# Reordering the first microseconds of a four-layer transformer kernel: layer-norm statistics and x chunks moved into the attention loop

## The chip, the cores and the metric

The kernel runs on one core of a Trainium2 chip. The metric is the device time of one execution in microseconds; less is better. A core has five engines that each work through their own instruction list in order and meet at semaphores: TensorE (PE), VectorE (DVE), ScalarE (ACT), GpSimd (POOL) and SyncE (SP), which here sends nearly all DMAs.

## What is computed

The input x has 32 batches of 128 tokens with 128 features; ctx has the same shape. Four layers follow one another:

```python
x = x + L0_xattn(layernorm(x), ctx, ctx)            # 16 heads of 8, rotary embedding on Q and K
x = x + L0_ffn(layernorm(x))                        # ternary weights, 128 -> 512 -> 128
x = x + L1_xattn(layernorm(x), ctx, ctx, mask)      # 16 query heads, 4 key heads, masks, norm of the output
x = x + L1_ffn(layernorm(x))                        # 8 experts, one chosen for each token
```

Of this only the start of the first attention layer is touched:

```python
def _layernorm(x, axis=-1, eps=1e-05):
    m = jnp.mean(x, axis=axis, keepdims=True)
    v = jnp.var(x, axis=axis, keepdims=True)
    return (x - m) / jnp.sqrt(v + eps)
Q = apply_rope(Q, cos_q, sin_q)
K = apply_rope(K, cos_k, sin_k)
scores = jnp.einsum('bhqd,bhkd->bhqk', Q, K) / math.sqrt(D_K)
attn = jax.nn.softmax(scores, axis=-1)
out = jnp.einsum('bhqk,bhkd->bhqd', attn, V)
```

## The kernel before

One batch (128 tokens) is one tile of x, and x stays in on-chip memory in the tensor XR. Two batches make a pair, and projections are made by pairs; scores, softmax and the product with V are made by batches. Pair 0 is batches 0 and 1, and so on.

**The loop.** All engines run the same software pipeline, `body_loop` (L253 and after), over a step number t. Each engine has a function `step(t, j)` with j = t % 6; steps -4 to 5 are written out, steps 6 to 23 are a hardware loop, and the last ones are written out again. Steps -8 to -5 stand ahead of `body_loop` on each engine (`for t in range(-AHEAD, START)`), and with other instructions between them they are the prologue. An engine's step t does work for different batches. On a pair p, ScalarE normalises (`normalise`, L931) at step 2p-8, TensorE transposes and projects Q at step 2p-6 and K at step 2p-5 (L499, L514), VectorE multiplies the projections by the cosine and sine tables right after (`rotate`, L1281), GpSimd adds the two products in the same step (`whole`, L1090), ScalarE casts the sum to bf16 one step later (`high`, L874), and GpSimd makes the two lower pieces (`cut`, L1101 to L1104, at steps 2p-5 for Q and 2p-4 for K). SyncE then sends the "stack" of the pair: DMAs from on-chip memory to on-chip memory that copy the pieces into the tensor Qs (six DMAs, L365, and one that clears a row, L367) at step 2p-4, and into Ks (six DMAs, L376) at step 2p-3.

On a batch b, TensorE makes the scores in two halves at step b-2 (`scores`, L558) and VectorE takes the negated row maxima of each half (`maxima`, L1316). GpSimd splits the maxima into bf16 pieces at step b-1 (`split_max`, L1112 to L1117), TensorE transposes them (`max_transpose`, L634), ScalarE copies them out (`evac_max`, L909), and SyncE sends them into a row of the stack (`max_rows`, L382), the last thing of its step b-1. At step b TensorE makes the transposed scores (`scoresT`), ScalarE the exponentials, TensorE the product with V.

Within TensorE's step the order is: scores half 0, product with V of the batch before, scoresT half 0, `max_transpose(t+1)`, `out_transpose`, `regroup`, the projection of Q (even t) or K (odd t), scoresT half 1, scores half 1 of batch t+2, product with V. Within VectorE's step: `add_out`, maxima half 0 of batch t+2, `denominators`, `norm_out`, `rotate`, maxima half 1 of batch t+2. Within GpSimd's step: `split_max(t+1)`, `cut`, `whole`. Within SyncE's step: the stack of Q (even t) or of K and the next chunk of ctx (odd t), then `max_rows(t+1)`.

**The statistics.** The norm of the first layer needs mean and variance of each tile. They are made in five groups of tiles, `GROUPS = ((0, 2), (2, 8), (8, 16), (16, 24), (24, 32))`. VectorE's `x_group(g)` waits for the chunk of x (four chunks of eight tiles, 512 KB each), then makes `bn_stats` (L1577) and `bn_aggr` (L1580) for each tile; GpSimd's `x_group(g)` waits for VectorE's and makes the reciprocal root and the shift in four instructions (L1065 to L1073). `normalise` of pair p waits for the group that holds the pair.

**The prologue before.** VectorE: group 0, then the stacks Ks[0], Ks[1], Ks[2] are filled with ones (L1585), group 1 ahead of step -7, group 2 ahead of step -6, group 3 ahead of step -5, group 4 after it. GpSimd: group 0, Qs[0], Qs[1], Qs[2] are cleared (L1156), then groups 1 to 4 in the same places. SyncE: chunk 0 of x, the first weights, the first chunk of ctx, and after step -7 nineteen loads of other weights and the x chunks 1, 2 and 3 (L327). At step -4 it waits until all six stacks are filled (`stacks_cleared`, 6) and sends the first stack.

Of the kernel before, what the change touches and what calls it, by code (L numbers as in the profile page):

```python
# [1 line left out]

# [1 line left out]

# [7 lines left out]
BF16 = mybir.dt.bfloat16  # L12
# [3 lines left out]
B, S, D = 32, 128, 128  # L16
HEADS, DK = 16, 8
# [9 lines left out]
AHEAD = 8  # L27
START = -4
# [14 lines left out]
GROUPS = ((0, 2), (2, 8), (8, 16), (16, 24), (24, 32))  # L43
# [13 lines left out]
def build(nc, a, out):  # L57
    ctx = ExitStack()
    with ctx:
        def sb(name, shape, dt=F32):  # L60
            return ctx.enter_context(nc.sbuf_tensor(name, shape, dt))
# [3 lines left out]
        def sem(name):  # L65
            if name not in sems:
                sems[name] = ctx.enter_context(nc.semaphore(name))
            return sems[name]
# [64 lines left out]
        Qs = [sb(f"Qs{i}", [128, HEADS // 2, PAIR], BF16) for i in range(3)]  # L133
        Ks = [sb(f"Ks{i}", [128, HEADS // 2, PAIR], BF16) for i in range(3)]
# [66 lines left out]
        blank = sb("blank", [128, EXPERTS, RW])  # L201
# [8 lines left out]
        before = sb("before", [128, 128], BF16)  # L210
# [30 lines left out]
        X_CHUNKS = 4  # L241
# [5 lines left out]

        body = {}

        def run(step, t):  # L250
            body["i"] = t // BODY
            step(t, t % BODY)

        def run_early(step, p):

            if isinstance(p, int) and p >= PAIRS - EARLY:
                run(step, p - (PAIRS - EARLY) - AHEAD)

        def body_loop(eng, step, first=-AHEAD, before=None):


            for t in range(first, BODY):
                run(step, t)
            with eng.Fori(1, NB) as i:
                body["i"] = i
                for j in range(BODY):
                    step(i * BODY + j, j)
            for t in range(NB * BODY, B + 3):
                if before and t in before:
                    before[t]()  # L270
                run(step, t)
# [52 lines left out]
        def _(sp):  # L324
            def load_x_chunk(c):
                w = B // X_CHUNKS
                sp.dma_start(X[:, c * w:(c + 1) * w, :], xd[:, c * w:(c + 1) * w, :]).then_inc(sem(f"x_loaded{c}"), 16)  # L327
# [69 lines left out]
            step = attention(0)  # L397
            for t in range(-AHEAD, START):
                run(step, t)
                if t == -AHEAD + 1:  # L400
                    for dst, src in other_loads:
                        sp.dma_start(dst, src).then_inc(sem("weights_loaded"), 16)
                    for c in range(1, X_CHUNKS):
                        load_x_chunk(c)
            sp.wait_ge(sem("stacks_cleared"), 6)
            sp.wait_ge(sem("zeros_set"), 1)
            body_loop(sp, step, START)
            for dst, src in expert_loads:
                sp.dma_start(dst, src).then_inc(sem("experts_loaded"), 16)

# [4 lines left out]
            sp.dma_start(blank[:, :, 2 * D:RW], a["tails"][DUMMIES * 128:].rearrange("(e p) w -> p e w", p=128)  # L415
                         ).then_inc(sem("tails_loaded"), 16)
            body_loop(sp, attention(1))

            sp.wait_ge(sem("tails_loaded"), 16)
# [419 lines left out]
        def _(act):  # L839
# [189 lines left out]
            step = attention(0)  # L1029
            for t in range(-AHEAD, START):  # L1030
                run(step, t)
            act.wait_ge(sem("weights_loaded"), LOADED)
            body_loop(act, step, START)
            early = attention(1)
# [7 lines left out]
        def _(pool):  # L1042
# [20 lines left out]
            def x_shift(name, tiles, n, index):  # L1063

                nc.gpsimd.tensor_tensor(xrs[:, tiles], xmv[:, tiles, 1], powers[:, 5:6].broadcast_to([128, n]), ALU.add  # L1065
                                        ).then_inc(sem(name + "_rstd"), 1)
                pool.wait_ge(sem(name + "_rstd"), 3 * index + 1)
                nc.gpsimd.tensor_tensor(xrs[:, tiles], xrs[:, tiles], powers[:, 0:1].broadcast_to([128, n]), ALU.pow
                                        ).then_inc(sem(name + "_rstd"), 1)
                pool.wait_ge(sem(name + "_rstd"), 3 * index + 2)  # L1070
                nc.gpsimd.tensor_tensor(xsh[:, tiles], xmv[:, tiles, 0], xrs[:, tiles], ALU.mult).then_inc(sem(name + "_rstd"), 1)
                pool.wait_ge(sem(name + "_rstd"), 3 * index + 3)
                nc.gpsimd.tensor_tensor(xsh[:, tiles], zero[:, 0:n], xsh[:, tiles], ALU.subtract).then_inc(sem(name), 2)  # L1073

            def x_group(g):

                lo, end = GROUPS[g]
                pool.wait_ge(sem("x0_stats"), 2 * end)
                x_shift("shifted0", slice(lo, end), end - lo, g)
# [72 lines left out]

            step = attention(0)
            x_group(0)
            for i in range(3):
                nc.gpsimd.memset(Qs[i][:], 0.0).then_inc(sem("stacks_cleared"), 1)  # L1156
            for t in range(-AHEAD, START):
                if t > -AHEAD:
                    x_group(t + AHEAD)
                run(step, t)  # L1160
            for g in range(START + AHEAD, len(GROUPS)):
                x_group(g)
            body_loop(pool, step, START)
            pool.wait_ge(sem("gate_unit"), 2)
            nc.gpsimd.tensor_tensor(wgn[:, 1:2], wgn[:, 0:1], powers[0:EXPERTS, 4:5], ALU.pow).then_inc(sem("gate_norm"), 1)
            early = attention(1)
# [62 lines left out]
        def _(dve):  # L1229
# [342 lines left out]
            def x_group(g):  # L1572

                lo, end = GROUPS[g]
                dve.wait_ge(sem(f"x_loaded{lo // (B // X_CHUNKS)}"), 16)
                for t in range(lo, end):
                    nc.vector.bn_stats(xst[:, t, :], X[:, t, :]).then_inc(sem("x0_stats"), 1)  # L1577
                dve.wait_ge(sem("x0_stats"), lo + end)
                for t in range(lo, end):
                    nc.vector.bn_aggr(xmv[:, t, :], xst[:, t, :]).then_inc(sem("x0_stats"), 1)  # L1580

            step = attention(0)
            x_group(0)
            for i in range(3):
                nc.vector.memset(Ks[i][:], 1.0).then_inc(sem("stacks_cleared"), 1)  # L1585
            dve.wait_ge(sem("first_loaded"), FIRST_LOADED)
            for t in range(-AHEAD, START):
                if t > -AHEAD:
                    x_group(t + AHEAD)
                run(step, t)  # L1590
            for g in range(START + AHEAD, len(GROUPS)):
                x_group(g)
            dve.wait_ge(sem("zeros_set"), 1)

            FW = (F1[:], F2[:].rearrange("p c n -> p (c n)"))
# [34 lines left out]
                sum_weights()  # L1630
                scale_norm()

            body_loop(dve, step, START, {B - 1: weights_ready, B: quantize, B + 2: fold_norm})
            nc.vector.tensor_tensor(wgs[:, 0, :], wgr[:], wgr[:], ALU.mult).then_inc(sem("gate_unit"), 1)
            dve.wait_ge(sem("gate_unit"), 1)
            nc.vector.tensor_reduce(wgn[:, 0:1], wgs[:, 0, :], AX.X, ALU.add).then_inc(sem("gate_unit"), 1)
# [95 lines left out]
```

## Time and profile before

| | |
|---|---|
| median of 3 runs | 695.83 us (694.47 to 696.17) |
| the profiled execution's own time | 697.29 us |
| its span in the profile | 695.5 us |
| PE busy | 561.4 us, 81% |
| DVE busy | 395.1 us, 57% |
| ACT busy | 353.4 us, 51% |
| POOL busy | 377.9 us, 54% |

The span runs from the first to the last instruction; what lies around it is 1.8 us. Times in the rows of the trace are microseconds from the start of the span. "Busy" counts the engine's own work, not waits or the issuing of DMAs, which is why SyncE ("SPq" in the trace, the queue from which it issues) has no share above. PE is TensorE's matmul row; two levels of its clock appear, and the share granted is shown in the views by stretch. Layer 0's attention fills the span from its start to about 223 us.

### The profile page before, as it was taken

What the parts mean: (1) busy time and instruction counts of PE and PEld (TensorE: products, weight loads), DVE (VectorE), ACT (ScalarE), POOL (GpSimd) and SP (SyncE); (2) the same over time, 40 slices, a digit from 0 to 9 for tenths busy, and PEclk for the clock granted to TensorE, in tenths of its full rate; (3) what the DMA queues carried; (4) which work ended last, traced back from release to release, by engine and by line L of the source; (5) the groups of instructions that cost most, each with busy time, mean ns of one, the idle gap of its engine ahead of it and who ended that gap; (6) DMA issues with size and microseconds to landing.
All of it is one profiled execution on the core that took longest, in us unless ns stands there. A gap on an engine that the chain in (4) does not pass through costs nothing.

```text
span 695.5 us, 19876 instructions
## 1 busy us (share of the span) xinstructions
PE 561.4 (81%) x6015; PEld 371.0 (53%) x6016; DVE 395.1 (57%) x1105; ACT 353.4 (51%) x839; POOL 377.9 (54%) x785
## 2 busy tenths in 40 slices
PE   1477989899875899959999999999882880499993
PEld 0345656666543799823444444444431450499993
DVE  6556667777765566434666666666643548044441
ACT  2136666776663456524655566565441520266662
POOL 6766556766710566645565655655324177255653
PEclk9999999999998799968999999999996855599997
DMA  6243333334327400022223222222100024233331
GB/s 185 77 108 87 98 95 90 101 97 104 96 51 233 113 2 0 17 80 73 64 59 80 70 58 69 77 56 62 39 7 2 9 104 158 75 93 94 98 99 31
DMA packets 97518, 54.02 MB, mean 78 GB/s; under 512 B 23138, under 2 KB 93538, under 8 KB 97458
## 3 DMA queue, kind: packets, MB, share of 16 engines
q1 hardware_dynamic: 94674, 46.45, 25.7%
q0 software_dynamic: 2784, 6.82, 2.7%
q8 instruction: 31, 0.51, 0.3%
q14 instruction: 29, 0.24, 0.1%
HBM read 19.79 MB, written 8.81 MB: 41 GB/s over the span
## 4 chain that ended last, share of the span: by engine, by line
PE 49%; SPq 24%; DVE 7%; POOL 6%; issue 6%; ACT 4%; DMA 2%; POOLq 0%; ACTq 0%; DVEq 0%
SPq L376 9%; SPq L365 9%; PE score L535 6%; PE scoreT L535 5%; PE bank L808 5%; PE bank L610 4%; ACT P L893 4%; PE scoreT L693 4%; DVE negmax L1316 4%; PE bank L703 4%; PE score L558 3%; PE scoreT L576 3%; PE scoreT L796 3%; SPq L382 2%; POOL expert_rows L1205 2%
## 5 line engine op out<-in xcount | busy, mean ns | idle before, releaser
L1316 DVE TENSOR_REDUCE negmax<-score 128x8 f32<-128x1024 f32 x128 | 156.5, 1223 | 96.9 <-PE score L558 76.6
L893 ACT ACTIVATE P<-scoreT 128x1024 f32<-128x1024 f32 x128 | 131.1, 1024 | 62.7 <-PE scoreT L576 42.6
L610 PE MATMUL bank<-P,Vc 128*32 128x128 f32 x2048 | 83.2, 281 | 0.4
L558 PE MATMUL score<-Ks,Qs 64*128 64x128 bf16 x1024 | 52.7, 224 | 18.9 <-DMA Ks<-piece 8.6
L558 PEld LDWEIGHTS score<-Ks,Qs 64*128 64x128 bf16 x1024 | 31.7, 97 | 56.1 <-issue 47.9
L1220 POOL DMA_INDIRECT out<-by x39 | 39.6, 1017 | 37.5 <-POOL by L1214 22.6
L610 PEld LDWEIGHTS bank<-P,Vc 128*32 128x32 f32 x2048 | 48.5, 110 | 14.3 <-ACT P L893 1.0
L1112 POOL TENSOR_TENSOR negp<-negmax,blank 128x16 bf16<-128x16 f32 x64 | 14.0, 219 | 74.8 <-DVE negmax L1316 74.8
L899 ACT COPY outs<-bank 128x256 f32<-128x256 f32 x64 | 23.7, 371 | 58.5 <-PE bank L610 58.5
L1101 POOL TENSOR_TENSOR piece<-full,piece 128x256 bf16<-128x256 f32 x64 | 42.8, 668 | 16.6 <-ACT piece L874 16.5
L535 PE MATMUL score<-mask,negI 128*128 128x512 bf16 x128 | 40.9, 403 | 11.0 <-issue 5.9
L1104 POOL TENSOR_TENSOR piece<-rest,piece 128x256 bf16<-128x256 f32 x64 | 44.5, 695 | 5.0
L1205 POOL DMA_INDIRECT expert_rows<-XR,sloti x32 | 32.4, 1013 | 25.0 <-DVE sloti L1489 15.9
L535 PE MATMUL scoreT<-negI,mask 128*128 128x512 bf16 x128 | 39.6, 392 | 7.2 <-ACT P L893 6.6
L808 PE MATMUL bank<-M,bhT 128*128 x312 | 44.2, 285 | 0.3 <-ACT bhT L1021 0.3
L1102 POOL TENSOR_TENSOR rest<-full,piece 128x256 f32<-128x256 f32 x64 | 42.7, 667 | 0.0
L874 ACT CAST piece<-full 128x256 bf16<-128x256 f32 x64 | 25.6, 400 | 32.6 <-DMA Qs<-blank 12.0
L808 PEld LDWEIGHTS bank<-M,bhT 128*128 128x128 f32 x312 | 38.6, 195 | 1.5 <-issue 0.4
L1021 ACT ACTIVATE bhT<-scoreT,Qs 128x128 f32<-128x128 f32 x104 | 29.7, 369 | 16.4 <-PE scoreT L796 16.4
L1551 DVE SCALAR_TENSOR_TENSOR by<-bank,XB 128x128 f32<-128x128 f32 x39 | 13.7, 351 | 42.1 <-PE bank L808 40.7
L1325 DVE RECIPROCAL rden<-bank 128x16 f32<-128x16 f32 x64 | 16.3, 255 | 36.5 <-PE bank L625 36.5
L1090 POOL TENSOR_TENSOR full<-rotA,rotB 128x256 f32<-128x256 f32 x32 | 23.2, 727 | 25.1 <-DVE rotB L1281 25.1
(195 smaller groups left out, 1236.0 us busy)
## 6 DMA issues: line engine op xcount, KB each, us to landing
Qs<-piece SPq DMA_DIRECT2D x192, 64.0 KB, 2.0
Ks<-piece SPq DMA_DIRECT2D x96, 64.0 KB, 2.0
ctxT<-in_ctxT SPq DMA_DIRECT2D x32, 128.0 KB, 2.3
XB<-expert_rows SPq DMA_DIRECT2D x39, 66.0 KB
XA<-expert_rows SPq DMA_DIRECT2D x39, 64.0 KB, 1.9
XR<-in_x SPq DMA_DIRECT2D x4, 512.0 KB, 4.8
Qs<-blank SPq DMA_DIRECT2D x32, 64.0 KB, 2.1
Qs<-negpT SPq DMA_DIRECT2D x64, 32.0 KB, 1.9
```

Source lines behind the costliest of these rows:

```text
L365: sp.dma_start(rows_of(Qs[b], s), piece[0][:, QSLOT[s], :]).then_inc(sem(f"q_stacked{L}{b}"), 16)
L376: sp.dma_start(rows_of(Ks[b], s)[:, 0:n_kv // 2, :], piece[1][0:n_kv * DK, KSLOT[s], :]).then_inc(sem(f"k_stacked{L}{b}"), 16)
L535: nc.tensor.matmul(out[:, r, :].rearrange("p (h n) -> p h n", h=HQ), of_stationary, of_moving.unsqueeze(1).broadcast_to([128, HQ, 128]), s ...
L558: mm = nc.tensor.matmul(SCORE[:, r, i * 128:(i + 1) * 128], Qs[pb][rows, h, tb * S:(tb + 1) * S], Ks[pb][rows, kv, tb * S:(tb + 1) * S], s ...
L610: mm = nc.tensor.matmul(PVOUT[VCOL * i:VCOL * (i + 1), half * 128:(half + 1) * 128], Vc[:, k % BODY, at:at + VCOL], P32[:, c, i * 128:(i + ...
L808: mm = nc.tensor.matmul(bank[4 + r][:, 0:D], bhT[r][:, c * 128:(c + 1) * 128], M2[:, bass.ds(e, 1), c:c + 1, :].rearrange("p o c n -> p (o ...
L893: nc.scalar.activation(P32[:, half * 2:half * 2 + 2, :], SCORET[:], ACT.Exp, scale=SCALE).then_inc(sem("exp_done"), 1)
L1101: nc.gpsimd.tensor_tensor(pc[0:m, 1, :], f, h, ALU.subtract).then_inc(sem(f"{nm}_pieces"), 1)
L1102: nc.gpsimd.tensor_tensor(r, f, h, ALU.subtract).then_inc(sem(f"{nm}_pieces"), 1)
L1104: nc.gpsimd.tensor_tensor(pc[0:m, 2, :], r, pc[0:m, 1, :], ALU.subtract).then_inc(sem(f"{nm}_pieces"), 1)
L1205: nc.gpsimd.indirect_dma_start(out=rows_d, out_offset=bass.IndirectOffsetOnAxis(ap=sloti[:, t:t + 1], axis=0), in_=XR[:, t, :], in_offset= ...
L1316: nc.vector.tensor_reduce(negmax[:, k % 2, :, half * HQ:(half + 1) * HQ], SCORE[:].rearrange("p r (h k) -> p r h k", h=HQ), AX.X, ALU.max, ...
```

## The change

- `body_loop` now also looks into its table `before` in the steps -4 to 5 (it did so only in the last ones).
- The statistics: group 1 is made right after group 0 on VectorE and GpSimd. The groups 2, 3 and 4 are made ahead of the steps 0, 2 and 4 on both engines (`later_groups`).
- SyncE sends the x chunks 1, 2 and 3 ahead of its steps -2, 0 and 2.
- VectorE fills Ks[0] and Ks[1] ahead of its steps and Ks[2] after step -6. GpSimd clears Qs[0] and Qs[1]; ScalarE clears Qs[2] after its step -6 with a copy of 2048 bf16 zeros.

The same instructions are executed as before, except that one GpSimd memset has become a ScalarE copy with a wait for the zeros.

```diff
+        def later_groups(x_group):
+
+            return {2 * g - 4: partial(x_group, g) for g in range(2, len(GROUPS))}
...
             for t in range(first, BODY):
+                if before and t in before:
+                    before[t]()
                 run(step, t)
...
                     for dst, src in other_loads:
                         sp.dma_start(dst, src).then_inc(sem("weights_loaded"), 16)
-                    for c in range(1, X_CHUNKS):
-                        load_x_chunk(c)
             sp.wait_ge(sem("stacks_cleared"), 6)
             sp.wait_ge(sem("zeros_set"), 1)
-            body_loop(sp, step, START)
+            body_loop(sp, step, START, {2 * c - 4: partial(load_x_chunk, c) for c in range(1, X_CHUNKS)})
...
             for t in range(-AHEAD, START):
                 run(step, t)
+                if t == -AHEAD + 2:
+                    act.wait_ge(sem("zeros_set"), 1)
+                    nc.scalar.copy(Qs[2][:].rearrange("p h s -> p (h s)"),
+                                   blank[:].rearrange("p e w -> p (e w)")[:, 0:HEADS * S // 2].bitcast(BF16)).then_inc(sem("stacks_cleared"), 1)
...
             x_group(0)
-            for i in range(3):
+            x_group(1)
+            for i in range(2):
                 nc.gpsimd.memset(Qs[i][:], 0.0).then_inc(sem("stacks_cleared"), 1)
             for t in range(-AHEAD, START):
-                if t > -AHEAD:
-                    x_group(t + AHEAD)
                 run(step, t)
-            for g in range(START + AHEAD, len(GROUPS)):
-                x_group(g)
-            body_loop(pool, step, START)
+            body_loop(pool, step, START, later_groups(x_group))
...
+            def clear(i):
+                nc.vector.memset(Ks[i][:], 1.0).then_inc(sem("stacks_cleared"), 1)
+
             x_group(0)
-            for i in range(3):
-                nc.vector.memset(Ks[i][:], 1.0).then_inc(sem("stacks_cleared"), 1)
+            x_group(1)
+            clear(0)
+            clear(1)
             dve.wait_ge(sem("first_loaded"), FIRST_LOADED)
             for t in range(-AHEAD, START):
-                if t > -AHEAD:
-                    x_group(t + AHEAD)
                 run(step, t)
-            for g in range(START + AHEAD, len(GROUPS)):
-                x_group(g)
+                if t == -AHEAD + 2:
+                    clear(2)
...
-            body_loop(dve, step, START, {B - 1: weights_ready, B: quantize, B + 2: fold_norm})
+            body_loop(dve, step, START, {**later_groups(x_group), B - 1: weights_ready, B: quantize, B + 2: fold_norm})
```

## Rows read from the trace of the kernel before

**Rows 1.** The page, part 4: the chain that ended last, by engine and line.
```profile
PE 49%; SPq 24%; DVE 7%; POOL 6%; issue 6%; ACT 4%; DMA 2%; POOLq 0%; ACTq 0%; DVEq 0%
SPq L376 9%; SPq L365 9%; PE score L535 6%; PE scoreT L535 5%; PE bank L808 5%; PE bank L610 4%; ACT P L893 4%; PE scoreT L693 4%; DVE negmax L1316 4%; PE bank L703 4%; PE score L558 3%; PE scoreT L576 3%; PE scoreT L796 3%; SPq L382 2%; POOL expert_rows L1205 2%
```

**Rows 2.** The chain of waits, 0 to 110 us: start, duration, what.
```profile
12.66 4.12 DMA XR<-in_x
16.80 1.65 DVE xst L1577 x8
...
27.86 1.65 POOL xrs L1068
```

**Rows 3.** Timeline of SyncE's queue: start, duration, line, out<-in, count [idle before <-releaser].
```profile
12.66 2.42 SPq L327 DMA_DIRECT2D XR<-in_x  x3
...
27.03 3.86 SPq L365 DMA_DIRECT2D Qs<-piece  x6
30.93 0.60 SPq L367 DMA_DIRECT2D Qs<-blank  x1
32.16 3.74 SPq L376 DMA_DIRECT2D Ks<-piece  x6
...
51.21 0.60 SPq L382 DMA_DIRECT2D Qs<-negpT  x1
...
78.84 1.48 SPq L347 DMA_DIRECT2D ctxT<-in_ctxT  x1
80.36 0.53 SPq L382 DMA_DIRECT2D Qs<-negpT  x1
```

**Rows 4.** Timeline of VectorE, prologue and the steps -1, 0, 2 and 4.
```profile
5.16 0.25 DVE L1580 BATCH_NORM_AGGREGATE xmv<-xst 128x2 f32<-128x6 f32 x2
5.78 1.76 DVE L1585 MEMSET Ks<- 128x2048 bf16 x1 [0.38 <-issue]
...
11.75 1.19 DVE L1577 BATCH_NORM_STATS2 xst<-XR 128x6 f32<-128x128 f32 x6
...
46.02 1.21 DVE L1316 TENSOR_REDUCE negmax<-score 128x8 f32<-128x1024 f32 x1
...
50.33 1.21 DVE L1316 TENSOR_REDUCE negmax<-score 128x8 f32<-128x1024 f32 x1
...
61.16 1.22 DVE L1316 TENSOR_REDUCE negmax<-score 128x8 f32<-128x1024 f32 x1
...
75.02 1.21 DVE L1316 TENSOR_REDUCE negmax<-score 128x8 f32<-128x1024 f32 x1
```

**Rows 5.** Timeline of GpSimd: the memsets, group 3 (first, last), a split (first).
```profile
7.05 5.29 POOL L1156 MEMSET Qs<- 128x2048 bf16 x3
...
22.39 0.20 POOL L1065 TENSOR_TENSOR xrs<-xmv,powers 128x8 f32<-128x8 f32 x1
...
24.74 0.20 POOL L1073 TENSOR_TENSOR xsh<-blank,xsh 128x8 f32<-128x8 f32 x1
24.89 0.67 POOL L1101 TENSOR_TENSOR piece<-full,piece 128x256 bf16<-128x256 f32 x1
...
42.05 0.22 POOL L1112 TENSOR_TENSOR negp<-negmax,blank 128x16 bf16<-128x16 f32 x1 [0.41 <-DVE negmax L1316]
```

**Rows 6.** Timeline of ScalarE: an exponential of 1024 columns, a copy of the maxima.
```profile
48.04 1.02 ACT L893 ACTIVATE P<-scoreT 128x1024 f32<-128x1024 f32 x1 [0.70 <-PE scoreT L585]
...
78.86 0.27 ACT L909 COPY negpT<-bank 128x128 bf16<-128x128 bf16 x1
```

**Rows 7.** Timeline of TensorE: first projection, first scores, transposes of maxima.
```profile
9.44 2.04 PE L499 MATMUL bank<-xnT,W 128*128 128x256 f32 x4 [0.51 <-issue]
...
37.43 0.61 PE L558 MATMUL score<-Ks,Qs 64*128 64x128 bf16 x8 [7.54 <-issue]
...
43.14 0.27 PE L634 MATMUL bank<-eyeb,negp 128*128 128x128 bf16 x1 [0.40 <-issue]
...
48.40 0.22 PE L634 MATMUL bank<-eyeb,negp 128*128 128x128 bf16 x1 [0.40 <-issue]
...
58.98 0.23 PE L634 MATMUL bank<-eyeb,negp 128*128 128x128 bf16 x1
...
72.01 0.29 PE L634 MATMUL bank<-eyeb,negp 128*128 128x128 bf16 x1
```

**Rows 8.** Stretches: each engine's busy time, TensorE's granted clock, DMA share, GB/s.
```profile
47.00:57.00 10.00, 7.74 (x130) 5.35 (x130) 7.01 (x11) 6.94 (x13) 7.16 (x17) 1.00 0.36 92
```

**Rows 9.** Stretches of 2 us, TensorE alone: busy, granted clock, DMA share, GB/s.
```profile
68.00:70.00 2.00, 0.43 (x4) 1.00 0.19 46
70.00:72.00 2.00, 1.87 (x32) 0.60 0.49 131
```

More of the change, by code:

```diff
@@ L1 @@
 from contextlib import ExitStack
+from functools import partial
 import numpy as np
```

## The prediction

> **What bounds the kernel now.** I read the page's chain first: SyncE's queue holds 24% of it, nearly all in the stack DMAs of layer 0 (L365, L376), the rest is spread over TensorE and others [rows 1]. The chain in order of time says what comes ahead of that: the load of x chunk 1 (12.66 to 16.80), VectorE's statistics of group 2, GpSimd's roots of three later groups, each of 1.65 us [rows 2], and then SyncE sends stack after stack, one DMA each 0.64 us, from 27.03 on [rows 3]. So up to the end of layer 0 SyncE's queue sets the pace, the later layers follow one another without slack, and what counts is when SyncE gets through step 5: at 80.36 it sends the maxima of batch 6 [rows 3]. What this send gains or loses I carry unchanged to the end. The sum is made against the profiled execution (697.29 us); the same difference is taken off the median of the runs, 695.83.
>
> **Part 1, the prologue.** VectorE ends group 0 at 5.41; group 1 now follows (its 12 instructions begin at 11.75 and end at 13.48, 1.73 us), so it ends at 7.15. Two memsets, one each 2.14 us with 1.76 busy and 0.38 ahead, end at 11.42 [rows 4]. TensorE's first Q projection ends at 11.48 as before [rows 7], so the rotation runs from 11.5 to 12.3 and not at 19.04, where it had stood behind the load of chunk 1 and group 2. TensorE's K projection follows at the same 2.04, VectorE's third memset lies beside it. GpSimd: group 1 from 7.2 to 9.5 (2.24 by its own run at 13.56), two memsets of 1.76 to 13.0 [rows 5], the sum of the rotation 0.72, ScalarE's cast 0.4, the three cuts 2.04: the first Q stack can be sent at 16.4, against 27.03, 10.6 us earlier. ScalarE's new copy has 2048 columns; by the 1.02 us of 1024 columns [rows 6] it takes about 1.9, and it lies from 10.4 to 12.4 where ScalarE waits for GpSimd's sum at 13.7. Its bounds are 1.0 and 2.6 us, and both are hidden. SyncE isn't held by the cleared stacks: the last one is VectorE's, at 14.4. The K stack goes right behind the Q stack, without the 0.63 us between 31.53 and 32.16 [rows 3], and ends at 24.8; the scores follow 1.53 us later as before (35.90 to 37.43 [rows 3, 7]). First scores: 26.3 against 37.43, 11.1 earlier. Steps -2 and -1 up to the last maxima of step -1 (47.23 [rows 4]) wait for nothing of SyncE and take the same 9.8 us: that point falls at 36.1. Call D(t) the end of the last maxima of step t: D(-1) is 36.1.
>
> **Part 2, the groups inside the loop.** Here the change pays. Ahead of step 0 VectorE makes group 2, 2.32 us (chunk 1 has been there for long), and only then can GpSimd begin its part, 2.55 us from 22.39 to 24.94 [rows 5], which stands in front of split_max. With the hops that is 4.95 us between D(t-1) and the split of maxima that were ready all the time. Behind the split waits TensorE, in order at max_transpose, and behind that on TensorE the projection, scores half 1 and so D(t). Behind GpSimd's split also wait the cuts, and SyncE behind both. This is a closed loop VectorE, GpSimd, TensorE, VectorE; it takes 5.1 to 5.2 us a step now (51.54 to 56.76; 76.23 to 81.33), about the pace of SyncE's DMAs, 10.1 us for two steps. Nothing in it absorbs 4.95 us; only SyncE has slack against it, about 2 us (the maxima of batch 1 left ScalarE at 49.22 and were sent at 51.21 [rows 3]).
>
> The steps 0, 2 and 4 one by one. D(t-1) to max_transpose is 1.17 now (47.23 to 48.40), and max_transpose to D(t) is 3.14 at step 0 and 3.40 at step 2 with the full clock [rows 4, 7]. The clock is the open point. TensorE will stand for about 4.6 us in each of the three steps. In the trace the granted share fell from 1.00 to about half, 1.2 GHz, at 70 us, after 2 us with 0.43 busy [rows 9]. At that level max_transpose to D(t) took 4.09 at step -1 and 4.22 at step 4 [rows 4, 7]. The Trainium skill, "TensorE: Matmul & The Clock Gate", section "The HAM clock gate", says that idleness lowers the clock and activity restores it; by that rule the low prices hold, which the row at 70 us bears out. I take the low prices for the even steps and 5.1 for the odd ones:
> - D(0) = 36.1 + 4.95 + 1.17 + 4.09 = 46.3; D(1) = 51.4
> - D(2) = 51.4 + 4.95 + 1.17 + 4.22 = 61.7; D(3) = 66.8
> - D(4) = 66.8 + 10.34 = 77.2
>
> The maxima of batch 6 leave ScalarE 2.9 us after D(4) (76.23 to 79.13 [rows 4, 6]), at 80.1, against a send at 80.36 now. SyncE's own work leads to the same place: the K stack of pair 4 waits for GpSimd until 66.8 + 4.95 + 1.05 (split) + 2.04 (cuts) and a hop = 74.9, and with 3.85 for six DMAs and 0.6 for the ctx chunk SyncE is through at 79.4, or at 80.3 if the 0.88 that L347 took above its usual 0.6 at 78.84 [rows 3] comes again. The gain is thus 0.1 to 0.3 us, and I take 0.3: of 11.1 us won ahead of the loop about 10.8 are given back in it.
>
> **Part 3, the chunks.** Three DMAs took 2.42 us of the queue in a row, 0.8 each [rows 3]; the next one was longer too, so 0.45 to 1.35 each. Chunk 1 is sent at step -2 and delays only stacks that are needed at D(-1) or later; chunks 2 and 3 fall at steps where SyncE then stands 2 to 3 us for the maxima. They cost nothing beside part 2. With that cover gone they would cost 1.4 to 4 us. Moving the chunks also takes them from in front of the first stacks, which is in part 1. The data of a chunk goes ahead of the Q stack behind it. The Trainium skill, "DMA: Bandwidth & Descriptors", section "Queues, rings and completion order", says that descriptors of one ring are consumed in order, which speaks against sending 512 KB between stacks; by it a stack behind a chunk would land up to some 2 us later, and the time would grow by that only where this stack is waited for last. The DMA engines are 0.36 busy in this stretch [rows 8], so the queue drains within the seven DMAs of a Q stack, and TensorE then stands for the split anyway; I add nothing.
>
> **Rivals.**
> - Full clock in steps 0 to 4. Then D(0) = 45.4, D(1) 50.5, D(2) 60.0, D(3) 65.1, D(4) 74.6; the maxima are there at 77.5, SyncE's own work ends at 77.7 to 78.6 and comes last. The gain is 1.8 to 2.7: 693.5. For it: the clock was at full level through shorter gaps. Against it: no gap of now is as long as 4.6 us. Chance 0.18.
> - The statistics hide after all. VectorE and GpSimd are busy only 7.0 and 7.2 of 10 us [rows 8], and a reader of the busy shares would put all six pieces into that idle time. Then the cost is the chunks alone, 2.4 us, and the gain 8 to 9: 687.5. Against it: the idle time lies inside the loop just traced, not beside it. Chance 0.09.
> - Slower, by the clock in the odd steps. If the low level lasts from the even step over the projection of the odd one, each odd step costs 5.95 (the 5.25 from 41.98 to 47.23 at low clock, and 0.7 for the transposes and products that step -1 doesn't have), and the even ones 0.5 more than above, since at 72 us the clock rose in the middle. That is 2 x 0.85 + 2 x 0.5 = 2.7 behind the forecast: 2.4 slower than before, 698.2. It decides when the low stretch is longer than some 5 us; the one now lasted from 70 to 74. Chance 0.15.
> - The prologue doesn't win what it should: some wait that the trace of before hides, a late weight or ctx, holds the first stack 3 us longer. The loop's price stays: 698.5. Chance 0.06.
>
> **How the numbers follow.** The forecast case, chance 0.52, is 695.83 - 0.3 = 695.5, its own range 693.8 to 697.2. A measurement of this kernel can tell about 0.3%, 2.1 us, from no change: below 693.7 is faster, above 697.9 slower. Faster gets the second rival, most of the first and a little of the forecast case: 0.25. Slower gets most of the third and the fourth and a little of the forecast: 0.18. The rest, 0.57, is the same. The range 691.5 to 699.0 leaves out the second rival and the ends of the last two.
>
> **What would show it.** In the trace after: the first stack at 16.4 and the first scores at 26.3 (part 1); in the steps 0, 2 and 4 eight bn_stats right after the maxima, then GpSimd's roots, then the split, with TensorE idle for 4 to 5 us before max_transpose and released by GpSimd (part 2); SyncE waiting for ScalarE's maxima or GpSimd's pieces three times; the granted clock at half in the steps 0, 2 and 4 or not (which rival); the send of the maxima of batch 6 at 80 us, whatever the start was. The prediction is wrong if TensorE isn't held by the split, if the clock stays at one level throughout, or if the 11 us don't come.

## The result and the profile after

The change makes the kernel slightly slower. Three comparisons, each against runs of the kernel before in the same series:

| | after, median us | before, median us | ratio, 95% interval |
|---|---|---|---|
| first | 698.86 | 694.63 | 1.0047 (1.0028 to 1.0065) |
| second | 697.69 | 697.03 | 1.0004 (0.9978 to 1.0030) |
| third | 697.02 | 695.04 | 1.0032 (1.0012 to 1.0053) |

So it is about 0.3%, 2 us, slower; two of the three intervals exclude no change, and all three exclude a gain of more than 0.3%. The prediction was 695.5 with most of the chance on "no change", and its forecast case had a gain of 0.3 us.

The profiled execution of after took 698.34 us with a span of 696.5, only 1.0 above the span of before. But a second trace of before (below) shows that the first had lost 2 us by chance in layer 1, so I compare by places and not by spans. The prediction had named one place, the send of the maxima of batch 6 by SyncE: 80.36 us in before [rows 3].

SyncE's queue in the trace of after: start, duration, line, out<-in, count. L372 and L374 are the Q stack, L383 the K stack, L389 the maxima, L334 an x chunk.

```profile
16.20 3.86 SPq L372 DMA_DIRECT2D Qs<-piece  x6
...
34.66 0.53 SPq L389 DMA_DIRECT2D Qs<-negpT  x1
35.24 0.59 SPq L334 DMA_DIRECT2D XR<-in_x  x1
35.94 3.74 SPq L372 DMA_DIRECT2D Qs<-piece  x6
39.73 0.58 SPq L374 DMA_DIRECT2D Qs<-blank  x1
41.43 0.53 SPq L389 DMA_DIRECT2D Qs<-negpT  x1
...
54.05 0.60 SPq L374 DMA_DIRECT2D Qs<-blank  x1
57.24 0.53 SPq L389 DMA_DIRECT2D Qs<-negpT  x1
...
69.92 0.60 SPq L374 DMA_DIRECT2D Qs<-blank  x1
73.93 0.53 SPq L389 DMA_DIRECT2D Qs<-negpT  x1
...
78.70 0.59 SPq L354 DMA_DIRECT2D ctxT<-in_ctxT  x1
81.78 0.53 SPq L389 DMA_DIRECT2D Qs<-negpT  x1
```

The first stack goes at 16.20, not 27.03: 10.8 us are won (forecast 10.6). Batch 0's maxima still have 10.9 of them (34.66 against 45.54). Then SyncE, which in before sends without a pause, stands still between the end of a Q stack and the maxima: 1.1 us at step 0, 2.6 at step 2 and 3.4 at step 4, and again ahead of 81.78. At that place after is 1.4 us behind. The view of waits of SyncE from 16 to 82 us names whom it waits for (us in total, times, longest):

```profile
SPq L389 <- ACT negpT L914: 12.2, 6, 3.4
```

VectorE in the steps -1 to 2 of after. L1322 is the row maxima, L1583 and L1586 the statistics of a group:

```profile
33.73 1.22 DVE L1322 TENSOR_REDUCE negmax<-score 128x8 f32<-128x1024 f32 x1
34.86 1.63 DVE L1583 BATCH_NORM_STATS2 xst<-XR 128x6 f32<-128x128 f32 x8
36.53 0.64 DVE L1586 BATCH_NORM_AGGREGATE xmv<-xst 128x2 f32<-128x6 f32 x8
...
44.02 1.23 DVE L1322 TENSOR_REDUCE negmax<-score 128x8 f32<-128x1024 f32 x1 [0.22 <-PE score L563]
...
49.17 1.21 DVE L1322 TENSOR_REDUCE negmax<-score 128x8 f32<-128x1024 f32 x1
...
60.01 1.22 DVE L1322 TENSOR_REDUCE negmax<-score 128x8 f32<-128x1024 f32 x1 [0.22 <-PE score L563]
```

and GpSimd over the same step 0, L1074 to L1082 the roots, L1121 the first instruction of the split of maxima that VectorE had finished at 34.95:

```profile
37.25 0.20 POOL L1074 TENSOR_TENSOR xrs<-xmv,powers 128x8 f32<-128x8 f32 x1 [2.37 <-DVE xmv L1586]
37.53 1.65 POOL L1077 TENSOR_TENSOR xrs<-xrs,powers 128x8 f32<-128x8 f32 x1
...
39.60 0.20 POOL L1082 TENSOR_TENSOR xsh<-blank,xsh 128x8 f32<-128x8 f32 x1
39.76 0.22 POOL L1121 TENSOR_TENSOR negp<-negmax,blank 128x16 bf16<-128x16 f32 x1
```

The split begins 4.81 us after the maxima; in before it began 0.07 after them (41.98 to 42.05 [rows 5]). TensorE in step 0 and in the steps 2 and 3 of after, with L639 the transposition of the maxima, L504 a Q projection (at the end of the even steps) and L519 a K projection (in step 3):

```profile
40.84 0.26 PE L639 MATMUL bank<-eyeb,negp 128*128 128x128 bf16 x1 [3.70 <-issue]
40.97 2.04 PE L504 MATMUL bank<-xnT,W 128*128 128x256 f32 x4
...
56.30 0.27 PE L639 MATMUL bank<-eyeb,negp 128*128 128x128 bf16 x1 [4.46 <-issue]
...
57.09 1.91 PE L504 MATMUL bank<-xnT,W 128*128 128x256 f32 x4
...
64.13 1.03 PE L519 MATMUL bank<-ctxT,W 128*128 128x256 f32 x4
```

TensorE idles 3.7 us at step 0 and 4.5 us at step 2 (and at step 4). Its granted clock in stretches of 2 us (busy, clock, DMA share, GB/s):

```profile
52.00:54.00 2.00, 0.00 (x0) 1.00 0.74 165
54.00:56.00 2.00, 0.00 (x0) 0.64 0.29 72
56.00:58.00 2.00, 1.70 (x7) 0.50 0.00 0
58.00:60.00 2.00, 2.00 (x23) 0.50 0.20 49
60.00:62.00 2.00, 2.00 (x24) 0.66 0.38 100
62.00:64.00 2.00, 1.71 (x36) 1.00 0.47 130
```

The clock falls from 2.4 to 1.2 GHz at 54.6, inside the gap, and rises again at 61.4; the work behind the gap (from 56.30 on) runs at the low level for 5.1 us. In step 4 the low level lasts from 71.6 to 78.5, which is 5.5 us of work, in step 0 from 37.5 to 44.3, 3.5 us of work (times from the same view in stretches of 0.2 us).

### The profile page after: what moved, and what is told of

Its sections match the earlier page's. It is cut to its first block, busy times and chain, and to the rows that moved or that the text cites. A ratio compares the mean times of both kernels' runs of the same rounds, so it can differ in the third digit from the quotient of the medians.

```text
span 696.5 us, 19875 instructions
## 1 busy us (share of the span) xinstructions
PE 559.1 (80%) x6015; PEld 371.5 (53%) x6016; DVE 395.4 (57%) x1105; ACT 354.7 (51%) x840; POOL 376.9 (54%) x784
## 4 chain that ended last, share of the span: by engine, by line
PE 51%; SPq 20%; DVE 7%; issue 7%; POOL 6%; ACT 5%; DMA 3%; POOLq 0%; ACTq 0%; DVEq 0%
SPq L372 8%; SPq L383 8%; PE scoreT L540 5%; PE bank L615 5%; PE score L540 5%; PE bank L813 5%; ACT P L898 4%; PE scoreT L698 4%; PE bank L708 4%; PE score L563 3%; DVE negmax L1322 3%; PE scoreT L581 3%; PE scoreT L801 3%; POOL expert_rows L1211 2%; SPq L389 2%
## 5 line engine op out<-in xcount | busy, mean ns | idle before, releaser
L1322 DVE TENSOR_REDUCE negmax<-score 128x8 f32<-128x1024 f32 x128 | 156.4, 1222 | 89.3 <-PE score L563 68.3
L898 ACT ACTIVATE P<-scoreT 128x1024 f32<-128x1024 f32 x128 | 131.1, 1024 | 63.8 <-PE scoreT L581 41.5
L563 PE MATMUL score<-Ks,Qs 64*128 64x128 bf16 x1024 | 52.2, 223 | 17.1 <-DMA Ks<-piece 9.6
L1121 POOL TENSOR_TENSOR negp<-negmax,blank 128x16 bf16<-128x16 f32 x64 | 14.1, 220 | 71.8 <-DVE negmax L1322 71.8
L813 PE MATMUL bank<-M,bhT 128*128 x312 | 44.3, 286 | 0.2 <-ACT bhT L1026 0.2
L1331 DVE RECIPROCAL rden<-bank 128x16 f32<-128x16 f32 x64 | 16.3, 255 | 40.6 <-PE bank L630 40.6
L1026 ACT ACTIVATE bhT<-scoreT,Qs 128x128 f32<-128x128 f32 x104 | 29.7, 369 | 16.4 <-PE scoreT L801 16.4
```

The source lines that it names most:

```text
L563: mm = nc.tensor.matmul(SCORE[:, r, i * 128:(i + 1) * 128], Qs[pb][rows, h, tb * S:(tb + 1) * S], Ks[pb][rows, kv, tb * S:(tb + 1) * S], s ...
L813: mm = nc.tensor.matmul(bank[4 + r][:, 0:D], bhT[r][:, c * 128:(c + 1) * 128], M2[:, bass.ds(e, 1), c:c + 1, :].rearrange("p o c n -> p (o ...
L898: nc.scalar.activation(P32[:, half * 2:half * 2 + 2, :], SCORET[:], ACT.Exp, scale=SCALE).then_inc(sem("exp_done"), 1)
L1322: nc.vector.tensor_reduce(negmax[:, k % 2, :, half * HQ:(half + 1) * HQ], SCORE[:].rearrange("p r (h k) -> p r h k", h=HQ), AX.X, ALU.max, ...
```

## The experiments

Theory A is the prediction's: the groups stand inside the closed loop of maxima, split, transposition, projection and next maxima. Rival B: the loss comes from the x chunks between the stacks, or the first layer is held elsewhere. A third question is the clock: what of the loss is due to it. All kernels but the first start from the kernel after. For each I give the send of batch 6's maxima, the last thing of SyncE's step 5, and the start of layer 1's first scores.

| kernel | batch 6 sent, us | layer 1's first scores, us | ratio to before |
|---|---|---|---|
| before, two traces | 80.36, 79.86 | 301.6, 300.7 | |
| after, three traces with e9 below | 81.78, 81.54, 81.13 | 303.4, 300.5, 301.7 | see above |
| e2 without groups 2 to 4 | 70.33 | 291.9 | 0.9895 (0.9858 to 0.9932) |
| e3 gaps filled with matmuls | 76.80 | 300.2 | 0.9967 (0.9940 to 0.9993) |
| e4 GpSimd's part behind the step | 72.47 | 293.1 | 0.9901 (0.9863 to 0.9938) |
| e6 VectorE's part alone | 70.14 | 292.3 | 0.9826 (0.9789 to 0.9863) |
| e7, e10 spread | 69.14, 68.20 | 295.4, 291.2 | 0.9880 (0.9844 to 0.9917), 0.9857 (0.9819 to 0.9894) |
| e8 chunks ahead of the stacks | 81.73 | 303.3 | one run, 698.26 us |
| e11 VectorE's part early | 72.35 | 293.5 | one run, 688.11 us |
| e12 split ahead of GpSimd's part | 72.02 | 293.4 | one run, 689.14 us |

The times of one kernel differ between chips and runs by more than these effects: before ran at 706.4 us (the series of e1 to e4), 697.0 (e5 to e8) and 695.0 (e9 to e12). Most of the step from 697 to 706 lies in the last layer, in eight DMAs with which SyncE writes blank rows (L423 in before): they took 16.0, 17.1, 16.1 and 17.2 us in the traces of e1 to e4, and 8.5 to 9.4 us in all others. The work behind them waits: GpSimd stood for 13.6 to 16.3 us behind its scatter of the token rows in those four traces, and for 7.0 to 7.4 in the others. Only the ratios within a series are compared, and the places in the first layer. Even the ratios carry some 0.5% between series: e2 and e6 send batch 6 within 0.2 us of each other, at ratios of 0.9895 and 0.9826.

**Before again.** No edit.

> The kernel before, unchanged, for a second trace. The profiled execution of before took 697.3 us while its other runs took 694.5 to 696.2, so about 2 us of it is chance. If the gain and loss of the change lie up to step 5, the send of the maxima of batch 6 stands again within 0.5 us of 80.4 and the 2 us are found later, behind 220 us. If chance lies in the first attention layer itself, that send moves by 1 to 2 us, and the comparison of the two traces at 80 us (81.8 against 80.4) is not to be trusted.

Batch 6 at 79.86, 0.5 us from the first trace; layer 1's first scores at 300.7 against 301.6. From there to the statistics behind layer 1 the first trace of before took 228.8 us, this one 226.8, and all others 226.0 to 227.5. So the comparison at batch 6 stands, and the 2 us by which the first profiled run of before lay above its median were lost in layer 1. The place "layer 1's first scores" carries chance of its own: from batch 6 to it the five traces of before and after took 219.0 to 221.6 us, and e7's 226.2.

**Without the groups 2 to 4.**

```diff
-            body_loop(pool, step, START, later_groups(x_group))
+            body_loop(pool, step, START, {-2: fill_scale, **later_groups(stand_in)})
...
-            body_loop(dve, step, START, {**later_groups(x_group), B - 1: weights_ready, ...
+            body_loop(dve, step, START, {B - 1: weights_ready, ...
```

`stand_in` waits for the x chunk and writes a constant shift.

> The kernel after without the statistics of groups 2 to 4: neither VectorE's nor GpSimd's instructions of them; GpSimd writes a constant scale and shift for those tiles instead (0.1 us each), so the numbers of batches 8 to 31 are not the reference's. The x chunks are still sent inside the loop. Theory A (the groups stand inside the closed loop and cost it 5 us each): the 12 us won ahead of the loop stay, less 1 to 3 us for the chunks and slack: 684 to 688 us, the batch 6 send at 70 to 73 us. Rival B (the loss comes from the chunks ahead of the stacks, or the first layer is held elsewhere): no less than 694 us.

```profile
70.33 0.53 SPq L389 DMA_DIRECT2D Qs<-negpT  x1
```

70.33, as theory A had it: the three groups cost 11.45 us at this place (81.78 - 70.33), against 10.8 won ahead of it. Rival B, which gives the first layer another bound, falls. The ratio 0.9895 is 7.3 us of 695, so 687.7, at the upper end of the 684 to 688 that I had expected. The traces show 9 to 10 us at both places; the noise between runs is of the size of the difference.

**The clock.**

```diff
                     scoresT(t, 0, j)
+                    if L == 0 and isinstance(t, int) and t in (0, 2, 4):
+                        pe.wait_ge(sem("k_rotated"), t + 6)
+                        for i in range(FILL):       # FILL = 60
+                            nc.tensor.matmul(QK[:, 0:128], eyeb[:], eyeb[:], start=True, stop=True)
                     max_transpose(t + 1)
```

> The kernel after with 60 additional bf16 matmuls of 128 columns on TensorE ahead of max_transpose in the steps 0, 2 and 4, into the projections' bank where their result is overwritten. They do no work that is used. They fill the gap in which TensorE waits for the split. If the granted clock at half level behind the gaps is what turned my 0.3 us gain into the loss, the steps lose 0.8 to 1.1 us each in the even and 0.7 in the odd ones: 3.5 to 5 us less than after, 694 to 695.5 us, with the clock at 1.00 from 44 to 85 us. If the clock isn't the cause, the time stays at 698 to 699.5 us.

The same view as above in this kernel:

```profile
54.00:56.00 2.00, 1.54 (x27) 1.00 0.42 94
56.00:58.00 2.00, 2.00 (x28) 1.00 0.18 45
58.00:60.00 2.00, 1.92 (x38) 1.00 0.28 72
60.00:62.00 2.00, 1.86 (x31) 1.00 0.39 100
```

and TensorE in its step 0, with L671 the added matmuls (60 of them took 3.52 us in the steps 2 and 4):

```profile
37.19 5.03 PE L671 MATMUL bank<-eyeb 128*128 128x128 bf16 x60
42.05 0.22 PE L640 MATMUL bank<-eyeb,negp 128*128 128x128 bf16 x1
```

With D(t) the end of the last maxima of step t, as in the prediction:

| | D(-1) | D(0) | D(1) | D(2) | D(3) | D(4) | batch 6 sent |
|---|---|---|---|---|---|---|---|
| forecast | 36.1 | 46.3 | 51.4 | 61.7 | 66.8 | 77.2 | 80.1 |
| after | 34.95 | 45.25 | 50.38 | 61.23 | 67.08 | 77.92 | 81.78 |
| e3, filled | 35.08 | 45.12 | 50.00 | 59.36 | 64.45 | 73.80 | 76.80 |

The clock stayed at 1.00 from 42 us on, the even steps 2 and 4 took 9.4 instead of 10.8 us, step 3 took 5.1 instead of 5.85, and batch 6 goes 5.0 us earlier. At step 0 the clock fell here too (0.50 from 38 to 40 us): there the added matmuls themselves ran at the low level, took 5.03 us, and held the transposition until 42.05, 1.2 us later than in after. That step gains only 0.3. That clock isn't the groups' doing: in e2, which has no groups in its loop, it stands at 0.50 from 38 to 42 us as well, behind two short waits of TensorE for stack DMAs. So nearly all of the gain comes from the gaps of steps 2 and 4. The timed ratio is 0.9967, 2.3 us under before (692.7, a little under the 694 to 695.5 that I gave). Across series that is some 4 us under after; at layer 1's first scores 1.7 us of the 5.0 are left (300.2 against 301.9, the mean of after), within the chance of that place. So the low clock behind the gaps costs about 5 us at batch 6, in one trace, and without it the kernel comes out below before; but it is a consequence of the gaps. The rest of the groups' price can be read inside this one series: e3 sends batch 6 6.5 us later than e2 and takes 6.2 us longer (704.14 against 697.92).

**GpSimd's part behind the step.**

```diff
-            body_loop(pool, step, START, later_groups(x_group))
+            body_loop(pool, step, START, None, later_groups(x_group))
```

The new last argument is a table `behind`, whose entries `body_loop` calls after `run(step, t)`.

> The kernel after with GpSimd's part of the groups 2, 3 and 4 behind the steps 0, 2 and 4 and not ahead of them; VectorE's part stays ahead. All work is done. Theory A: the split of step t no longer waits for VectorE's statistics and the roots, only the next split is late by what GpSimd has no idle time for, at most 2 us instead of 5: 689 to 692 us. Rival B: 697 us or more, as the same work is done by the same engines.

All work done, and batch 6 goes at 72.47, 9.3 us earlier than in after. The order alone holds it. The ratio 0.9901 is 6.9 us of 695, 688, a little under the range I gave. Rival B falls again. TensorE's longest gaps ahead of a transposition are 1.8 us here, and yet the clock falls once more, inside the one that ends at 57.53:

```profile
56.00:58.00 2.00, 0.47 (x3) 0.74 0.41 108
58.00:60.00 2.00, 2.00 (x7) 0.50 0.43 119
```

**After again, twice.** No edit.

> The kernel after, unchanged, again. The start of layer 1's first scores stood at 301.6 and 300.7 us in two traces of before and at 303.4 in that of after. If these 2 to 2.7 us are the change's and not chance, it stands at 303 to 304 again, and the ratio is again above 1, 1.002 to 1.006.

> The kernel after, unchanged, in five rounds, to settle the size of its change. The ratio to before was 1.0047 (1.0028 to 1.0065) in the first comparison and 1.0004 (0.9978 to 1.0030) in a second one. The traces put the change's own part at the send of batch 6's maxima: 81.8 and 81.5 against 80.4 and 79.9, 1.2 to 1.9 us later, 0.2 to 0.3%. If that is all, the ratio is 1.000 to 1.005; a ratio above 1.005 needs a second cause behind 90 us.

Batch 6 at 81.54 and 81.13. Layer 1's first scores at 300.5 and 301.7, not at 303 to 304: the 2 us that the first trace of after had lost behind 90 us were chance. The mean of the three traces at batch 6 is 81.48 against 80.11 of before: 1.4 us, 0.2%, are shown in the first layer. That is 1.0020; two of the three intervals contain it, and the first (1.0028 to 1.0065) lies above it. Whether the change costs anything more than the 1.4 us, these runs can't tell.

**VectorE's part alone.**

```diff
-            body_loop(pool, step, START, later_groups(x_group))
+            body_loop(pool, step, START, {-2: fill_scale, **later_groups(stand_in)})
```

GpSimd's roots are left out, with a constant scale and shift in their place.

> The kernel after with VectorE's statistics of groups 2 to 4 where the change has them, and GpSimd's part left out (a constant scale and shift in its place, which wait only for the x chunk). Theory A in its strong form (all 4.95 us of a group are on the loop): VectorE's 2.3 us cost too, batch 6 is sent at 75 to 77. In its weak form (only what stands ahead of the split counts, VectorE's part costs because GpSimd waits for it there): the split starts at once, and VectorE's 2.3 us delay only half 0 of the next scores, which TensorE reaches later anyway: batch 6 at 70.3 to 72, as without the groups (70.33).

```profile
70.14 0.53 SPq L389 DMA_DIRECT2D Qs<-negpT  x1
```

The same as without any group (70.33). The weak form holds: 3 x 2.3 us on VectorE cost nothing themselves. They cost only through GpSimd, which stands in front of a ready split and waits for them.

**VectorE's part early.** The other half: VectorE's groups ahead of the steps -3 and -2, the chunks behind the weights, GpSimd's part where the change has it.

```diff
-            body_loop(dve, step, START, {**later_groups(x_group), B - 1: weights_ready, ...
+            body_loop(dve, step, START, {-3: partial(x_group, 2), -2: last_groups, B - 1: weights_ready, ...
```

> VectorE's statistics ahead of the steps -3 and -2, chunks behind the weights, but GpSimd's part ahead of the steps 0, 2 and 4 as in after. It parts the 4.95 us of a group into the two engines' shares. Theory A: GpSimd no longer waits for VectorE and starts its 2.55 us while it would wait for the maxima; per group the split is late by 1.3 to 2.2 us instead of 5, batch 6 goes at 72 to 76. If GpSimd's part alone were the price, whatever is ahead of it, batch 6 goes at 78 or later.

```profile
35.33 0.20 POOL L1076 TENSOR_TENSOR xrs<-xmv,powers 128x8 f32<-128x8 f32 x1
...
37.68 0.20 POOL L1084 TENSOR_TENSOR xsh<-blank,xsh 128x8 f32<-128x8 f32 x1
37.84 0.22 POOL L1123 TENSOR_TENSOR negp<-negmax,blank 128x16 bf16<-128x16 f32 x1
```

GpSimd starts right behind its own work, ahead of the end of the maxima at 35.66, and the split is late by 2.2 us instead of 4.8. Batch 6 goes at 72.35. So GpSimd's 2.5 us alone cost about 2 us in all at batch 6 (72.35 against 70.33), VectorE's alone nothing, and one behind the other, ahead of the split, 11.45. The parts don't add up. The loop has slack: without the groups its five steps from D(-1) to D(4) take 30.4 us in e2 and 29.0 in before, not five times 5.1, since TensorE there also waits for SyncE's stacks. Three delays of 4.8 us and the 5.0 of the clock make 19.4, of which 11.45 arrive at batch 6. That the slack swallows the short delays nearly whole is my reading; no run measures it by itself. The clock doesn't part short from long by falling or not: it falls with short gaps too (0.50 from 38 to 44 us and from 66 to 68 in e11, where no gap is longer than 1.8 us), so what e3 prices is the low stretches of after's steps 2 and 4 alone.

**Split ahead of GpSimd's part.** `x_group` called between `split_max` and `cut` in the steps 0, 2 and 4.

```diff
                     split_max(t + 1, j + 1)
+                    if isinstance(t, int) and t in split_first:
+                        split_first[t]()
```

> The kernel after with GpSimd's part of the groups between split_max and cut of the steps 0, 2 and 4, and nothing else changed: the split no longer waits, but the cuts and with them the K stacks do, for VectorE's statistics and the roots. Theory A: the loop over the maxima is free of the 5 us, SyncE waits about 1 to 3 us for the pieces of each of three K stacks, which is less than for the maxima, batch 6 goes at 72 to 77. If the cuts are as much on the path as the split, batch 6 goes at 80 or later.

72.02. Two pieces of work swapped on one engine gives back 9.8 us. SyncE now waits for pieces of the K stacks instead, twice by 1.1 us from 34 to 75 us; I had expected three waits of 1 to 3.

**Chunks ahead of the stacks.** The chunks undone, everything else as in after.

```diff
+            for c in range(1, X_CHUNKS):
+                load_x_chunk(c)
             sp.wait_ge(sem("stacks_cleared"), 6)
             sp.wait_ge(sem("zeros_set"), 1)
-            body_loop(sp, step, START, {2 * c - 4: partial(load_x_chunk, c) for c in range(1, X_CHUNKS)})
+            body_loop(sp, step, START)
```

> The kernel after with one part undone: the x chunks 1 to 3 are sent ahead of the first stack, after the weights, and not inside the loop. The statistics stay where the change has them. If the chunks between the stacks cost nothing (my forecast), batch 6 is sent at 81.3 to 82.3 as in after (81.78). If a stack queued behind a chunk is waited for, it is sent 1 to 3 us earlier. If the chunks ahead of the first stack delay it, the first scores come later than 26.1 by up to 3 us.

```profile
13.04 2.23 SPq L334 DMA_DIRECT2D XR<-in_x  x3
16.11 3.92 SPq L372 DMA_DIRECT2D Qs<-piece  x6
...
81.73 0.53 SPq L389 DMA_DIRECT2D Qs<-negpT  x1
```

81.73 against 81.78: the chunks between the stacks cost nothing, as forecast. And moving them there had gained nothing either. Once the rotation of pair 0 no longer stands behind chunk 1, SyncE idles from 13 to 16 us, the three DMAs fit in, and the first scores start at 26.06 with 1.5 MB ahead of the stacks, and at 26.09 without. The ring order that the prediction took from the Trainium skill, "DMA: Bandwidth & Descriptors", section "Queues, rings and completion order", had no effect on the time in either place.

**Everything in idle time.** The reasons point to a better version: chunks behind the weights, VectorE's groups where it stands idle (18.5 to 20.6 and 21.4 to 26.7 us), GpSimd's group 2 ahead of step -3, the groups 3 and 4, which are needed only at the steps 8 and 16, behind the steps 1 and 4.

```diff
-            body_loop(pool, step, START, later_groups(x_group))
+            body_loop(pool, step, START, {-3: partial(x_group, 2)}, {1: partial(x_group, 3), 4: partial(x_group, 4)})
```

> The kernel after with all of its work, placed by the theory: x chunks 1 to 3 sent right after the weights (SyncE's queue stands idle from 13.0 to 16.2), VectorE's group 2 ahead of step -3 and groups 3 and 4 ahead of step -2 (it stands idle from 21.4 to 26.7), GpSimd's group 2 ahead of step -3, group 3 behind step 1 and group 4 behind step 4. Theory A: nothing waits ahead of a split for two engines, batch 6 is sent at 69 to 72, layer 1's first scores at 291 to 293 and the time is 1.0 to 1.4% under before. Rival B (chunks in front of the stacks cost what they did before, 4 us or more): first scores of layer 0 at 29 or later, and less than 0.7%.

> The kernel with all work placed in idle time (chunks behind the weights, VectorE's groups ahead of the steps -3 and -2, GpSimd's ahead of step -3 and behind the steps 1 and 4) once more, beside after and before of the same call: 0.986 to 0.990 of before, the send of batch 6 at 69 to 70.

```profile
68.20 2.03 SPq L391 DMA_DIRECT2D Qs<-negpT  x1
```

Batch 6 goes at 69.14 and 68.20, and the kernel takes 0.9880 and 0.9857 of before: 687.9 against 697.0 us, 684.1 against 695.0. That is 9 to 11 us faster than before and 10 to 13 faster than after in the same series, with the same instructions as after. The second send and ratio lie just under what I expected of e10 (69 to 70, 0.986). In e7 layer 1's first scores came only at 295.4: one DMA of maxima took 3.58 us at 198.31 where 1.9 is usual; e10, the same kernel, has them at 291.2.

## Why the prediction was wrong, point by point

**The prologue (part 1): right.** First stack at 16.20 (forecast 16.4), first scores at 26.09 (26.3), ScalarE's copy 1.88 us (1.9) and hidden. The rival "the prologue doesn't win" is out.

**The end of step -1: 1.15 us better.** The first scores gave 0.2 of it. The rest: I had carried over 9.8 us from before for the steps -2 and -1, and in after they took 8.86. In after the clock rose inside step -1 (0.50 until 30 us, 0.84 from 30 to 32), and the K projection took 1.10 instead of 2.05 us. In before the rows of step -1 have the durations of the low level, though the view by stretch prints 1.00 there. The K projection of that step, and the stretch in which it begins:

```profile
43.26 2.05 PE L514 MATMUL bank<-ctxT,W 128*128 128x256 f32 x4
...
42.00:44.00 2.00, 1.48 (x11) 1.00 0.40 104
```

A K projection takes 1.03 us where the clock has risen, so the 1.00 that the view prints ahead of its first change of level (70 us in before) doesn't fit the durations, and the prediction's 4.09 "at that level" rested on durations alone. Its argument against the first rival, "no gap of now is as long as 4.6 us", doesn't hold either: TensorE stood for 7.54 us ahead of the first scores [rows 7], and the durations behind that gap are those of the low level.

**The groups in the loop (part 2): the mechanism right, the clock behind it too small.** D(t-1) to the split was 4.8 at all three steps (forecast 4.95), and D(t-1) to max_transpose 5.9 (forecast 6.12). Step 0 took 10.30 us (forecast 10.21) and step 1 5.13 (5.1). Three terms were too small:
- The even steps 2 and 4: 10.85 and 10.84 instead of 10.34. The term is max_transpose to D(t), priced at 4.22 and measured at 4.93 and 4.94. I had taken it from the row at 72.01 [rows 7], where the clock rose in the middle of the projection (1.57 us for it, not the 1.91 of after).
- Step 3: 5.85 instead of 5.1. Not its own K projection was slow (1.03 us at 64.13, clock 1.00). What TensorE still does for step 2 behind the last scores, among it the V projection, ran at the low level and ended late: ScalarE's copy of it begins 0.9 us behind D(2), in e3 0.1.
- From D(4) to the send: 3.86 instead of 2.9, in the same way. ScalarE works in order and first waited for this V projection of step 4; its copy begins 1.0 us behind D(4), in before 0.1 behind it, and from there to the copy of the maxima both take 2.53 us:

```profile
78.96 0.37 ACT L891 COPY Vc<-bank 128x256 f32<-128x256 f32 x1 [1.66 <-PE bank L534]
...
81.49 0.27 ACT L914 COPY negpT<-bank 128x128 bf16<-128x128 bf16 x1
```


Together 0.51 + 0.50 + 0.75 + 0.96 = 2.72, less the 1.15 of step -1 and with 0.1 of steps 0 and 1: the send at 81.78 and not at 80.1. Thus the chosen case failed in one step, the sentence "I take the low prices for the even steps and 5.1 for the odd ones": the low clock was priced too low inside the even steps, and what it delays behind D(t) was put at nothing. The third rival had the even steps right (0.5 more each) and the cause, but not the place of the rest. It asked for 0.85 in each odd step by a slow K projection; step 1 lost nothing, step 3 lost 0.75 with its projection at the full clock, and 0.96 came behind D(4). That its 2.7 equals the 2.72 above is luck, and so is 698.2 beside the measured 698.86, since it left out the 1.15 won at step -1 and the first comparison was the slowest of three. I had put it at 0.15, on the ground that the low stretch of before lasted from 70 to 74 (70.4 to 73.8 in finer stretches). That stretch had begun while TensorE was working; in after the low stretches of steps 2 and 4 last 6.8 us, and 5.1 and 5.5 of them fall on work of the loop. In e3 all of this is gone: its even steps 2 and 4 take 9.4, step 3 takes 5.1, and the send comes 3.0 behind D(4).

**The loop's pace: misread, without effect on the sum.** I gave the loop of before 5.1 to 5.2 us a step. That holds for the steps 1 and 5; the steps 2, 3 and 4 took 5.6, 6.2 and 7.6. So "nothing in it absorbs 4.95 us" was wrong, as the 11.45 us of e2 show. The sum is built from after's own terms, where the groups set the pace, and step 1 took 5.13.

**The chunks (part 3): right** (e8), and moving them into the loop was needless once group 1 came first.

**The statistics hide after all:** wrong for the order of the change, but the rival's number, a gain of 8 to 9 us, is about what one gets at batch 6 when the same instructions stand elsewhere (7.6 to 11.9 us against before in e4, e7, e10 and e12). The busy shares were no lie; the order was at fault.

## What to carry to other kernels

In a software pipeline, look for the closed loop over the engines and ask of each moved instruction whether it stands in front of an instruction of the loop that is ready. Two engines' pieces in a row ahead of one ready instruction cost their sum plus what the clock takes behind the gap, less the slack of the loop; the same pieces behind that instruction cost little (2 us here). And when a change opens a gap on TensorE, price the work behind it at the low clock, as far as the trace shows the low level to last (here 3.5 to 5.5 us of work), and follow what that work delays on the other engines into the next step.

## What the runs showed of the hardware

- The fall of the clock costs more than the gap: the gaps of 4.5 us in the steps 2 and 4 cost nearly 5.0 us on top of themselves at batch 6 (e3), although TensorE isn't busy throughout (7.74 of 10 us in before [rows 8]).
- Even 60 matmuls right behind the start of a gap didn't keep the clock up at step 0, where TensorE had also stood for 2.4 us just before. They took 5.03 us instead of 3.52; by 42 us the clock was back, and the projection behind them took 1.08 us instead of 2.04.
- Short gaps don't keep the clock up for certain: in e2, e4 and e11, where TensorE never stands longer than 2.4 us between 30 and 70 us, it was at 0.50 for 2 us or more at least once.
- Three DMAs of 512 KB issued 3 us ahead of the stacks did not delay stacks of 64 KB behind them: first scores 26.06 against 26.09.
- Chance is local: one DMA of 3.58 instead of 1.9 us, 2 us in layer 1 of before, 8 us in eight DMAs of the last layer. Three traces of after and two of before, read at the place where the change acts, told 1.4 us apart (81.13 to 81.78 against 79.86 to 80.36); the totals needed 27 runs of after in three comparisons for about the same.
